# Unsorted chunks ahead of pair 10, transposes two ahead of products, and where the eight unsorted groups stand

## The reference

```
q, k, v = gelu(n @ W1 + b1) @ W2 + b2      for each of the three; n = layernorm(x)
scores  = tril(q k^T) / sqrt(256 * 512)    (no softmax)
x1      = x + layernorm(scores @ v) * ln_w + ln_b
tile    = argmax over 8 tiles of pe[row] . sign(tile_sigs)      (by position only)
out     = x1 + layernorm(x1) @ W[tile]^T + b[tile]
```

## Time and profile before

| | before |
|---|---|
| median of 3 runs | 312.41 us (311.78 to 313.00) |
| the profiled execution | 312.93 us, its span 311.2 us |
| PE busy | 289.2 us, 93% |
| DVE busy | 237.7 us, 76% |
| ACT busy | 189.0 us, 61% |
| POOL busy | 176.7 us, 57% |
| PE busy from 260 to 270 us | 5.54 of 10 us, granted clock 0.80 |
| PE busy from 270 to 280 us | 8.11 of 10 us, granted clock 0.69 |
| PE busy from 290 to 300 us | 9.77 of 10 us, granted clock 1.00 |

### The profile page before, as it was taken

One profiled execution on the slowest core, in us unless ns is written; L12 is line 12 of the kernel. 1 busy time (PEld: TensorE's weight loads), 2 busy tenths in 40 slices (PEclk: granted clock), 3 DMA queues, 4 the chain that ended last, 5 costly groups with the idle time before them and its releaser, 6 DMA issues.

```text
span 311.2 us, 5456 instructions
## 1 busy us (share of the span) xinstructions
PE 289.2 (93%) x1806; PEld 254.4 (82%) x1806; DVE 237.7 (76%) x539; ACT 189.0 (61%) x380; POOL 176.7 (57%) x238
## 2 busy tenths in 40 slices
PE   8999998998999999999999999999999995788991
PEld 6789887997898989889788988898988984677870
DVE  5769788899889978967995896788587687245661
ACT  2565775776676876776678658769675436053410
POOL 6881532370685568475737545584577578545552
PEclk9999999999999999999999999999999999579997
DMA  7909950012021120121031000260224413911110
GB/s 223 233 22 333 350 175 27 0 37 66 0 75 67 36 72 2 68 70 39 10 127 54 20 0 2 73 199 2 88 95 134 154 58 127 312 53 67 50 42 17
DMA packets 24209, 27.83 MB, mean 89 GB/s; under 512 B 4659, under 2 KB 22068, under 8 KB 24118
## 3 DMA queue, kind: packets, MB, share of 16 engines
q1 hardware_dynamic: 15910, 13.68, 14.7%
q0 software_dynamic: 3296, 8.64, 8.0%
q10 hardware_dynamic: 4976, 5.16, 4.9%
HBM read 13.95 MB, written 14.44 MB: 91 GB/s over the span
## 4 chain that ended last, share of the span: by engine, by line
PE 79%; DVE 11%; issue 4%; ACT 3%; POOL 1%; ACTq 0%; POOLq 0%; DVEq 0%
PE ring L493 42%; PE o_ps L493 11%; PE s_ps L493 6%; PE w_ps L493 5%; PE ring L502 2%; PE ring L521 2%; PE sc_ps L606 2%; PE ring L764 1%; ACT xn L986 1%; PE sc_ps L764 1%; PE sc_ps L604 1%; DVE xnT L1166 1%; DVE st L1152 1%; DVE xres L1245 1%; PE w_ps L649 1%
## 5 line engine op out<-in xcount | busy, mean ns | idle before, releaser
L493 PE MATMUL ring<-xnT,w_sp 128*128 128x512 f32 x288 | 73.5, 399 | 3.7 <-DVE hT L1171 1.7
L493 PEld LDWEIGHTS ring<-xnT,w_sp 128*128 128x128 f32 x288 | 51.9, 189 | 16.0 <-issue 3.4
L892 ACT ACTIVATE ring<-ring,b_cols 128x512 f32<-128x512 f32 x48 | 31.7, 660 | 27.2 <-PE ring L493 25.8
L493 PE MATMUL ring<-hT,w_sp 128*128 128x512 f32 x192 | 46.7, 397 | 0.2 <-DVE hT L1171 0.2
L1171 DVE TENSOR_TENSOR hT<-ring,hT 128x512 fp32r<-128x512 f32 x48 | 32.5, 681 | 14.0 <-ACT hT L895 12.3
L493 PEld LDWEIGHTS ring<-hT,w_sp 128*128 128x128 f32 x192 | 35.2, 188 | 8.8 <-DVE hT L1171 0.9
L1717 POOL DMA_INDIRECT sorted_rows<-xres,slot_i x30 | 31.2, 1039 | 8.5 <-issue 6.5
L1782 POOL DMA_INDIRECT out_dram<-slot_rows x22 | 22.0, 999 | 17.6 <-DVE slot_rows L1464 12.0
L1683 POOL TENSOR_TENSOR vtok<-v,vtok 128x512 fp32r<-128x512 f32 x14 | 17.9, 1289 | 24.5 <-ACT vtok L912 24.5
L895 ACT CAST hT<-ring 128x512 fp32r<-128x512 f32 x48 | 28.2, 587 | 1.5
L1245 DVE SCALAR_TENSOR_TENSOR xres<-cen,rs,xres 128x256 f32<-128x256 f32 x32 | 24.1, 762 | 1.9 <-issue 1.6
(11 more groups left out here) (241 smaller groups left out, 683.7 us busy)
## 6 DMA issues: line engine op xcount, KB each, us to landing
sorted_rows<-blank ACTq DMA_DIRECT2D x1, 5032.0 KB, 20.8
xt<-x SPq DMA_DIRECT2D x7, 512.0 KB, 3.4
slot_rows<-sorted_rows SPq DMA_DIRECT2D x22, 136.0 KB
w_stage<-tile_w SPq DMA_DIRECT2D x8, 256.0 KB, 3.3
h<-sorted_rows SPq DMA_DIRECT2D x15, 136.0 KB
xt<-x SPq DMA_DIRECT2D x2, 256.0 KB, 3.0
hT<-position_table POOLq DMA_DIRECT2D x1, 512.0 KB, 9.4
sorted_rows<-xres,slot_i POOLq DMA_INDIRECT x30
```

The costliest lines, as they stand in the source:

```text
L493: last = te.matmul(o, lhs[k][a], rhs[k][c], start=start and k == 0 and i == 0, stop=stop and k == n - 1 and i == 2, skip_group_check=check)
L892: nc.scalar.activation(full, ring[(2 + m) % 3][:, :], ACT.Gelu, bias=b1c[:, m // 2, m % 2:m % 2 + 1]).then_inc(gelu, 1)
```

## The change

`LATER` goes from 12 to 10, so the unsorted chunks have place 10 and pair m from 10 on has place m+1. The four lists are put in another order to match. On PE a pair's transposes stand two ahead of its products, groups 0 to 4 stand between pairs and groups 5 to 7 at the end (before: one group ahead of each of the pairs 12 to 17, and two at the end). On ACT the norm of pair m+2 follows the rounding of pair m. On DVE `pair_rest(8)` goes ahead of `x1_stats`, `pair_rest(9)` ahead of `pair_out(8)`, and so on. On POOL `rstd_out(LAST, (2, 3))` goes ahead of `rows_sorted(LAST, (0, 1))`, and `slots(14)` behind `rstd_x1(LAST, (2, 3))`. No instruction is added or taken away.

```diff
--- before.py
+++ after.py
@@ -54,7 +54,7 @@
 FIRST = (STEPS - 2) * CH - NT + 1
 EARLY = (STEPS - 1) * CH - NT + 1
 
-AMID, INNER, MIDDLE, LATER = 1, 5, 8, 12
+AMID, INNER, MIDDLE, LATER = 1, 5, 8, 10
 CLASSES = PER
 NOWHERE = 2 * NB * T
 FILLS = 14
@@ -863,15 +863,28 @@
             pair_products(9)
             pair_transposes(10)
             pair_transposes(11)
+            dense_products(0, 0)
+            pair_transposes(12)
+            dense_products(0, 1)
             pair_products(10)
-            pair_transposes(12)
+            pair_transposes(13)
             pair_products(11)
-            for m in range(LATER, PAIRS):
-                pair_transposes(m + 1)
-                dense_products((m - LATER) // 4, (m - LATER) % 4)
-                pair_products(m)
-            for i in range(PAIRS - LATER, NT):
-                dense_products(i // 4, i % 4)
+            dense_products(0, 2)
+            pair_transposes(14)
+            pair_products(12)
+            pair_transposes(15)
+            pair_products(13)
+            dense_products(0, 3)
+            pair_transposes(16)
+            pair_products(14)
+            pair_transposes(17)
+            pair_products(15)
+            dense_products(1, 0)
+            pair_transposes(18)
+            pair_products(16)
+            pair_products(17)
+            for g in range(1, NT // 2):
+                dense_products(1, g)
 
         @block.scalar
         def _(act):
@@ -1113,15 +1126,14 @@
             pair_rounded(8)
             pair_norm(9)
             pair_rounded(9)
+            pair_norm(PAIRS)
             pair_norm(10)
-            pair_rounded(10)
+            pair_rounded(PAIRS)
             pair_norm(11)
-            pair_rounded(11)
-            pair_norm(PAIRS)
-            pair_rounded(PAIRS)
             for m in range(LATER, PAIRS):
-                pair_norm(m)
                 pair_rounded(m)
+                if m + 2 < PAIRS:
+                    pair_norm(m + 2)
 
         @block.vector
         def _(dve):
@@ -1478,6 +1490,10 @@
                 nc.vector.scalar_tensor_tensor(out=dense_rows(e)[:, 0:C], in0=o_ps[i % 2][:, t % 2 * C:t % 2 * C + C],
                                                scalar=onehot[:, t, j:j + 1], in1=dense_rows(e)[:, 0:C],
                                                op0=ALU.mult, op1=ALU.add).then_inc(dense_done, 1)
+
+            def dense_pair(e, g):
+                dense_out(e, 2 * g)
+                dense_out(e, 2 * g + 1)
 
             def last_masked(j):
                 dve.wait_ge(scores, CH * LAST + (2, 1, 3, 3)[j])
@@ -1619,27 +1635,37 @@
             pair_out(6)
             pair_rest(7)
             x1_final(LAST, (2, 3))
+            pair_rest(8)
             x1_stats(LAST, (2, 3))
             x1_var(LAST, (2, 3))
             pair_out(7)
-            pair_rest(8)
+            pair_rest(9)
             pair_out(8)
-            pair_rest(9)
             pair_out(9)
+            pair_rest(PAIRS)
             pair_rest(10)
+            dense_pair(0, 0)
             pair_rest(11)
+            dense_pair(0, 1)
             pair_out(10)
-            pair_rest(PAIRS)
+            pair_rest(12)
             pair_out(11)
-            for m in range(LATER, PAIRS):
-                pair_rest(m)
-                g = m - LATER
-                dense_out(g // 4, g % 4 * 2)
-                dense_out(g // 4, g % 4 * 2 + 1)
-                pair_out(m)
-            for g in range(PAIRS - LATER, NT):
-                dense_out(g // 4, g % 4 * 2)
-                dense_out(g // 4, g % 4 * 2 + 1)
+            dense_pair(0, 2)
+            pair_rest(13)
+            pair_out(12)
+            pair_rest(14)
+            pair_out(13)
+            dense_pair(0, 3)
+            pair_rest(15)
+            pair_out(14)
+            pair_rest(16)
+            pair_out(15)
+            dense_pair(1, 0)
+            pair_rest(17)
+            pair_out(16)
+            pair_out(17)
+            for g in range(1, NT // 2):
+                dense_pair(1, g)
 
         @block.gpsimd
         def _(pool):
@@ -1819,11 +1845,11 @@
             rstd_out(LAST, (0, 1))
             slots((11, 12))
             rstd_x1(LAST, (0, 1))
+            rstd_out(LAST, (2, 3))
             rows_sorted(LAST, (0, 1))
-            rstd_out(LAST, (2, 3))
-            slots((13, 14))
+            slots((13,))
             rstd_x1(LAST, (2, 3))
-            slots(range(15, SLOTS))
+            slots(range(14, SLOTS))
 
 
 def position_table(seq, dim):
```

## The result

The changed kernel takes 309.16 us (median of five runs, 308.54 to 310.33) against 312.41 us; the ratio is 0.9898 (95% interval 0.9872 to 0.9924). Forecast were 302.1 us in a range of 300.6 to 306.6. The profiled execution took 308.54 us, against 312.93 us before: 4.39 us less where the sum had 10.3. The same kernel run once more beside other kernels (e8) gave 309.62 us, 0.99 (0.9861 to 0.9939).

What follows compares the result with a forecast made beforehand. PE was taken as the bound where fed, starved and then slow between 261 and 277 us. PE's end falls from 304.35 to 294.05, 10.3 us less: profiled 302.6, median 302.1 us, range 300.6 to 306.6.

Steps and rivals of the forecast that it cites:

- the sum: PE's tail: 261.35 + 30.1 us of work + waits of 0.7, 1.65 and 0.25 = 294.05, 10.3 us less.
- POOL's power early: Tail start: power ahead of two scatters lets x1 of the last chunks start on DVE at 259.3, 1.6 us earlier.
- 1.65 in all: Around transposes 11 and group 0: two PE waits summing to 1.3 to 1.9 us, taken as 1.65.
- The 0.25 us before pair 17: Late tail: a PE wait of 0.25 us where a group's output on DVE stands in the pair's chain.
- Three groups at the end: End of tail, instead of two groups: no PE cost, as group 5's output ends inside group 6's 1.41 us.
- one of my signs of being wrong: Tail: ACT waiting for a load of slots 23 to 28 would show the forecast wrong.
- the rival in which the clock halves: From about 267 us, half clock for 10 us loses 4.35 us, giving 306.5 us; chance 0.18.
- POOL's scatters: Tail on POOL: 16 scatters from 273.9 end at 294.2, costing nothing as long as one takes 1.27 us.
- Groups 0 and 1 around transposes 12: From group 0 on: at least 1.90 us of PE covers a pair's 1.5 us chain, removing 0.32 us per pair and 0.86.
- the 2.6 that I gave waits in all: PE's tail: the waits left, 0.7 before products 9, 1.65 around transposes 11 and group 0, 0.25 before pair 17.
- POOL becomes the bound: Tail: scatters at 1.34 to 1.40 us or later outputs end POOL 1 to 2 us later, 303 to 304 us; chance 0.12.

Runs made afterwards that it cites:

- e8: The changed kernel run once more, unaltered, beside other kernels: 309.62 us, ratio 0.99.
- e10: Changed kernel with six unsorted groups spread evenly between pairs and two at the end: 309.92 us, ratio 0.9896.
- e3: Changed kernel without the output scatters of slots 14 to 36, so those rows are never written: 299.66 us, ratio 0.9557.
- e17: Changed kernel with a 128x256 addition on POOL ahead of the scatters of pairs 7 to 14 and none after: 2.3% faster than the kernel before.
- e9: Changed kernel with a 128x512 addition (about 1.3 us) on POOL between the scatters of one pair and the next: 311.79 us, ratio 0.9932.
- e5: Changed kernel with SP's plain stores to fixed places instead of the 23 scatters of slots 14 to 36: 300.33 us, ratio 0.9625.
- e4: Changed kernel with PE's products, from pair 10 on, also waiting until the group before last has been posted: 309.98 us, ratio 0.9899.
- e2: Changed kernel with all pairs multiplied by tiles at fixed addresses instead of a tile number in a register: 306.99 us, ratio 0.981.
- e14: Changed kernel with a 128x256 addition on POOL between the scatters of one pair and the next; about 306 us expected, and it came out as expected.
- e15: Changed kernel with a 128x64 addition on POOL behind each single scatter; 304.5 to 306.5 us expected, and it had the time expected.
- e13: Changed kernel with a 128x128 addition on POOL between pairs' scatters; 306 to 309 us expected if pause length counts, and it came out so.
- e1: Kernel before with only the early POOL and DVE edits, up to products 9: 310.59 us, ratio 0.9911.
- e16: Changed kernel with a 128x256 addition on POOL ahead of pairs 7 to 12 only; 306 to 309 us expected, and it came out as expected.
- e7: Changed kernel with a 128x512 addition on POOL in place of each scatter of slots 14 to 36, rows not written: 300.07 us, ratio 0.9624.
- e6: Changed kernel with scatters of slots 14 to 36 bounded to drop every row but row 0: 308.17 us, ratio 0.9862.

## Why the prediction was wrong

**Right.** POOL's power early: x1 at 259.71 (forecast 259.3), products 8 without a wait, products 9 after 0.37 us (0.7), transposes 11 and group 0 after 0.55 and 0.54 (1.65 in all). The 0.25 us before pair 17 is there as well, 0.18 us (292.91 to 294.63 for products that take 1.54); the wait of 0.26 before products 12 was not in the sum. Three groups at the end cost nothing. Of the loads only that of slot 26 was late: ACT waited 0.55 us ahead of its second norm of pair 12 (269.64), where the kernel lets it wait for nothing but that load; this was one of my signs of being wrong, but PE lost nothing by it.

**Right, with luck.** The clock held until 288 us, through four short waits, and fell behind 3.73 us. That it held early was not safe: e10, whose lists are the same up to there, has 1.11 us before transposes 11 and the clock at 0.50 behind them, and so has e3 behind 1.30. Yet e17 with 1.09 us kept it. So the rival in which the clock halves was a real one.

**The step that failed** is "POOL's scatters": that they cost nothing as long as one takes 1.27 us. They do take 1.28 (1.35 at most), and I looked only at when POOL would be through. That a full POOL queue could hold back what PE tells the others was in no rival: posts came up to 4.61 us late, and PE waited 3.73 us. With it fell the step "Groups 0 and 1 around transposes 12", in which a pair's chain of 1.5 us is covered by 1.90 us of PE: a cover of 0.4 us does nothing against a post 4 us late.

**Its price.** From transposes 9 to the end of the last group the changed kernel took 39.10 us (261.46 to 300.56), the sum had 33.06. The steps from transposes 17 to products 16 hold 5.66 us above their plain durations: 3.97 with the wait, 0.50 and 1.01 at half clock, and the 0.18 before pair 17. Those before hold 3.00, against the 2.6 that I gave waits in all. The rest is 0.47 us that this execution was later ahead of transposes 9. PE so ended 6.5 us late, and the end behind it gave 0.6 back: 5.9 us, from 302.6 to 308.54.

**The end.** I had the last output and its store set the end. What sets it is the last scatter: the span ends 5.88 us behind that scatter's end in both kernels (305.32 to 311.2; 300.93 to 306.8) and 5.9 in e9 (303.71 to 309.6), and so in every run with all scatters but e8, where the last output on DVE is 3.9 us behind the last scatter and sets the end. Without scatters it ends 2.2 us behind DVE's last output (e5: 294.93 to 297.1). That did no harm to the sum, as scatter and output moved together, but it hid what POOL's end is worth. The rival "POOL becomes the bound" had the right engine and another mechanism: trains ran at 1.28 us each, and POOL's last one is the end in the changed kernel too, but because late posts made its outputs late (slot 21 started at 276.84, where I had 273.9). One reading in that rival was off: the gaps of the scatters between 265 and 270 us were 1.34, 1.40 and 1.28 us.

**Open.** Why indirect DMAs hold back PE's increments and, as far as there are records, nobody else's isn't shown. Nor is it shown whether the increment alone is late or the matmul's last bytes too; the trace gives the matmul's end only by a model. The late posts were hardly smaller where PE had less queued (e4, up to 4.0 us) or no registers (e2, 4.5). How dense scatters must be isn't shown either: two in 3.09 us had no post over 0.5 us late (e14), two in 2.98 us still had 2.2 (e15), two in 2.87 us had 3.8 (e13), and a train of four was enough for 1.3 us in e1, while one of eight did nothing in e17. So dense scatters are needed, and something else decides whether they do harm.

## What to carry to other kernels

When an engine is "released late" though its producer's last instruction ended long before, look at the time at which the increment was posted, and at what GpSimd does just then. Trains of indirect DMAs look harmless on GpSimd's own row and may cost TensorE's consumers microseconds: spread them, or insert a short operation of GpSimd between them, but count its time, since the last indirect DMA may also set the end. A slack of a few tenths of a microsecond in a hand-written order should be checked against such delays before a forecast builds on it.

## What the runs showed of the hardware

- TensorE's semaphore increments were posted up to 4.8 us behind the matmul's end in the trace (e16), while GpSimd issued indirect DMAs of 128 rows 1.28 us apart, mostly six to eight in a row. One train of eight (e17) went without it. With a pause of 0.5 us for every two of them it nearly vanished (e14), and with plain stores by SyncE (e5) or additions on GpSimd (e7) it was gone.
- Writing almost no rows (e6) left posts up to 3.8 us late.
- While scatters run, records of increments are missing from the trace: 14 of ScalarE's 34 in the changed kernel's tail, 1 of 33 without the scatters (e3).
- The span ends 5.9 us behind the last indirect DMA, or 2.2 us behind the last VectorE output that a plain store carries, whichever is later.
- Waits of TensorE of 1.30 and 0.54 us (e3), and of 1.11 and 0.54 us (e10), were followed by the granted clock at 0.50; waits of 1.09 and 0.54 us (e17) left it at 1.00.
